# The combination of the second expert layer's rows moved unit by unit into the first steps of the last attention, with a scale of its own for four tiles

## The reference

```
    # third block, feed-forward: two experts of eight per token
    router_logits = jnp.einsum('bth,eh->bte', x, router_w)
    topk_values, topk_indices = jax.lax.top_k(router_logits, TOP_K)
    topk_weights = jax.nn.softmax(topk_values.astype(jnp.float32), axis=-1).astype(x.dtype)
    ...
    mixed_output = jnp.sum(topk_expert_outputs * topk_weights[..., None], axis=2)
    ...
    x = x + _L2_ffn_ref(_layernorm(x, axis=-1), ...)
    x = x + _L3_xattn_ref(_layernorm(x, axis=-1), ctx_1024, ...)   # 16 heads of 8, 64 tokens a sequence
    x = x + _L3_ffn_ref(_layernorm(x, axis=-1), ...)
```

## Time and profile before

| | |
|---|---|
| median of 3 runs | 1655.08 us (1648.52 to 1657.23) |
| profiled execution, its own time | 1662.0 us |
| its span in the profile | 1660.1 us |
| TensorE busy | 1342.2 us (81%) |
| VectorE busy | 1039.3 us (63%) |
| ScalarE busy | 925.4 us (56%) |
| GpSimd busy | 619.1 us (37%) |
| fetches of L1520, issue to landing | 5.7 us median, 6.8 at most |
| barrier ahead of the last attention | over at about 1270.3 us |
| first maxima of the last attention | 1282.70 us |
| last work of the last attention's steps | about 1462 us |

### The profile page before, as it was taken

One profiled execution on the slowest core, in us unless ns is written; L12 is line 12 of the kernel. 1 busy time (PEld: TensorE's weight loads), 2 busy tenths in 40 slices (PEclk: granted clock), 3 DMA queues, 4 the chain that ended last, 5 costly groups with the idle time before them and its releaser, 6 DMA issues. The chain is left out here.

```text
span 1660.1 us, 43005 instructions
## 1 busy us (share of the span) xinstructions
PE 1342.2 (81%) x16821; PEld 1121.6 (68%) x16821; DVE 1039.3 (63%) x2573; ACT 925.4 (56%) x2096; POOL 619.1 (37%) x604
## 2 busy tenths in 40 slices
PE   4799999986899997998259965777772988788994
PEld 3588877864688886787126653776661776687994
DVE  5677777764453423787879978533326788853445
ACT  3465655543345443897636634555445777634884
POOL 2233333221000000332258850677770225644662
PEclk9899999998999999898579997999995888978997
DMA  9200000009995000340000001111113001001335
GB/s 316 57 18 19 19 18 18 3 2 145 177 148 68 1 2 13 91 126 29 1 20 18 18 2 52 41 48 50 48 49 113 18 11 41 28 31 55 95 90 172
DMA packets 143528, 94.10 MB, mean 57 GB/s; under 512 B 55776, under 2 KB 130273, under 8 KB 142817
## 3 DMA queue, kind: packets, MB, share of 16 engines
q1 hardware_dynamic: 134368, 72.86, 20.3%
q0 software_dynamic: 8960, 18.50, 3.5%
HBM read 51.20 MB, written 40.12 MB: 55 GB/s over the span
## 5 line engine op out<-in xcount | busy, mean ns | idle before, releaser
L400 POOL TENSOR_TENSOR wide_probs<-wide_probs,wide_key_mask 128x512 f32<-128x512 f32 x64 | 82.7, 1315 | 187.5 <-ACT wide_probs L521 187.5
L1536 POOL DMA_INDIRECT moe_x_rows<-moe_rows,moe_source x72 | 80.5, 1118 | 74.7 <-DVE moe_source L1632 53.1
L739 POOL MEMSET attn_v_bd<- 128x576 f32 x2 | 1.2, 618 | 266.1 <-POOLq L163 266.1
L769 POOL TENSOR_TENSOR attn_col_bd<-attn_col_t,group_mask_sb 128x1024 f32<-128x1024 f32 x32 | 60.8, 1899 | 100.0 <-ACT attn_row_t L966 100.0
L2234 DVE TENSOR_TENSOR moe_hidden<-banks,moe_gate 128x256 f32<-128x256 f32 x104 | 43.6, 423 | 84.3 <-ACT moe_gate L2433 82.3
L3046 ACT ACTIVATE moe_router<-banks,moe_rb_sb 128x512 f32<-128x512 f32 x64 | 41.4, 689 | 91.7 <-PE banks L3150 67.5
L2069 POOL DMA_INDIRECT moe_results<-moe_y_rows,moe_x_rows x72 | 69.0, 958 | 51.7 <-issue 29.3
L843 DVE TENSOR_REDUCE attn_top<-banks 128x32 f32<-128x2048 f32 x32 | 73.1, 2283 | 21.0 <-PE banks L1027 21.0
L1542 POOL DMA_INDIRECT moe_results<-moe_y_rows,moe_dest x72 | 74.6, 1036 | 22.8 <-issue 20.7
L995 ACT ACTIVATE attn_probs<-attn_probs 128x1024 f32<-128x1024 f32 x64 | 66.0, 1054 | 28.3 <-DVE attn_probs L872 26.7
L2656 PE MATMUL banks<-moe_xb_t,moe_staged 128*128 128x128 f32 x576 | 76.1, 275 | 0.0
(11 more groups left out here) (434 smaller groups left out, 4362.6 us busy)
## 6 DMA issues: line engine op xcount, KB each, us to landing
moe_rows<-route_empty_sb SPq DMA_DIRECT2D x8, 2624.0 KB, 23.0
attn_ctx<-in_ctx_t SPq DMA_DIRECT2D x48, 128.0 KB, 2.1
moe_x_rows<-moe_rows SPq DMA_DIRECT2D x72, 66.0 KB, 1.9
moe_pack_sb<-in_moe_pack SPq DMA_DIRECT2D x8, 578.0 KB, 3.9
moe_w_sb<-in_moe_w SPq DMA_DIRECT2D x2, 2048.0 KB, 10.6
moe_hot<-moe_results SPq DMA_DIRECT2D x16, 256.0 KB, 5.7
moe_until_back<-moe_results SPq DMA_DIRECT2D x16, 256.0 KB, 5.9
moe_pack_sb<-in_moe_pack SPq DMA_DIRECT2D x9, 384.0 KB, 4.3
```

Of the source, the lines that this page charges most:

```text
L400: nc.gpsimd.tensor_tensor(probs[b.parity][:, :, h2], probs[b.parity][:, :, h2], keys, ALU.mult).then_inc(masked, 1)
L769: nc.gpsimd.tensor_tensor(col_bd[:], col_t[u.parity][:].unsqueeze(1).to_broadcast(shape), w["group_mask"][:].unsqueeze(2).to_broadcast(sha ...
L1536: nc.gpsimd.indirect_dma_start(x_rows[s % GATHERS][:], None, rows, bass.IndirectOffsetOnAxis(ap=source[:, s:s + 1], axis=0)).then_inc(gath ...
```

## The change

The eight units of the combination are no longer worked off by the second expert layer. SP still fetches them there, ahead of the barrier. The buffer they land in and the weights move to `core.carried`, which lives until the end; the last attention, which follows, uses the same space later for its expert blocks (`staged`, `x_rows`). Scaling, adds and bn_stats are now written into the last attention: unit 0 ahead of everything, with a norm of its own for tiles 0 to 3; units 1 to 3 behind the constant, with a norm for tiles 4 to 15; units 4 to 7 at the end of VectorE's steps 2 to 5, and behind the last a norm for tiles 16 to 31. There are three norms where there were two. ScalarE's `xhat` waits for the first, the second (from step 2) or the third (from step 8).

```
-                dve.wait_ge(y_taken, len(order))
-                dve.wait_ge(weighted, 1)
-                for u in range(UNITS):
...
+                def combine(u):
+                    part = slice(u * UNIT, (u + 1) * UNIT)
+                    dve.wait_ge(late_scaled, u + 1)
+                    nc.vector.tensor_tensor(core.x[:, part], core.x[:, part], core.late_in[:, 0, part], ALU.add).then_inc(late_half, 1)
+                    dve.wait_ge(late_half, u + 1)
+                    nc.vector.tensor_tensor(core.x[:, part], core.x[:, part], core.late_in[:, 1, part], ALU.add).then_inc(late_added, 1)
+                    dve.wait_ge(late_added, u + 1)
+                    for t in range(UNIT):
+                        ins = nc.vector.bn_stats(core.stats[:, u * UNIT + t], core.x[:, u * UNIT + t])
+                    ins.then_inc(late_stats, 1)
+
+                def first_scale(first_unit, units):
+                    tiles = slice(first_unit * UNIT, (first_unit + units) * UNIT)
+                    dve.wait_ge(late_stats, first_unit + units)
+                    norm_scale(core, dve, tiles)
+                    shifts(tiles)
...
-                shifts(FIRST_HALF)
+                combine(0)
+                first_scale(0, 1)
                 arrived(core, dve, "const", name, "moe3", "route", "dispatch")
                 dve.wait_ge(const_made, 1)
                 nc.vector.tensor_tensor(constant[:], y_of(0), w["attn3_bo"][:], ALU.add).then_inc(const_ready, 1)
-                norm_scale(core, dve, SECOND_HALF)
-                shifts(SECOND_HALF)
                 nc.vector.memset(d.seen[0][:], 0.0).then_inc(seen_made, 1)
+                for u in range(1, 4):
+                    combine(u)
+                first_scale(1, 3)
...
+                    if 4 <= s + 2 < UNITS:
+                        combine(s + 2)
+                        if s + 3 == UNITS:
+                            first_scale(4, 4)
...
+                def scale_late(u):
+                    act.wait_ge(core.late_landed[u], 2 * DMA_INC)
+                    for k in range(2):
+                        for t in range(UNIT):
+                            at = u * UNIT + t
+                            ins = nc.scalar.activation(core.late_in[:, k, at], core.late_in[:, k, at], ACT.Copy,
+                                                       scale=core.late_weight[:, k, at:at + 1])
+                    ins.then_inc(late_scaled, 1)
+
+                scale_late(0)
...
+                    if s == 1:
+                        scale_late(2)
...
                     if inside(s):
+                        act.wait_ge(norm_ready, 1 if s < 2 else 2 if s < 8 else 3)
...
+                    if s == 0:
+                        scale_late(1)
+                    elif s == 1:
+                        scale_late(3)
+                        scale_late(4)
...
+                    if 5 <= s + 3 < UNITS:
+                        scale_late(s + 3)
...
                     if inside(c):
+                        pool.wait_ge(late_added, c // 2 + 1)
```

More of the change, by code:

```diff
@@ L1484, in sparse_experts @@
         y_made, y_taken = sem("y_made"), sem("y_taken")
[L1485 to L1486 removed]
+        y_landed = core.late_landed
         rank_bank, table_bank = core.bank[7], core.bank[6]
@@ L1748, in _ @@
                         ins.then_inc(hid_ready, 1)
-                act.wait_ge(weighted, 1)
-                for u in range(UNITS):
-                    act.wait_ge(y_landed[u], 2 * DMA_INC)
-                    for k in range(1 if gated else 0, 2):
-                        for t in range(UNIT):
-                            at = u * UNIT + t
-                            ins = nc.scalar.activation(y_in[:, k, at], y_in[:, k, at], ACT.Copy, scale=weight[:, k, at:at + 1])
-                    ins.then_inc(scaled, 1)
             @block.tensor
```

57 lines of the change are left out of this document (16 added, 41 removed).

## The result

Twenty executions of each kernel on one chip: before 1655.15 us median (1647.01 to 1663.46), after 1660.73 us (1653.95 to 1668.22). The ratio is **1.0037, 95% interval [1.0022, 1.0053]**: 5.6 us slower. The likeliest case was the right one in its mechanism and too large in size: the forecast had put 0.49 on slower by more than 0.5% and 0.43 on less than that, and the measured 0.37% lies in the second.

What follows compares the result with a forecast made beforehand. VectorE was taken as the engine to count, waiting only 12.7 of 65.2 us. +8.0 at the third reciprocal, less 0.92, gave +7.1; with 1.9 for TensorE's clock +9.0, so 1664.1 us, range 1654 to 1672.

Steps and rivals of the forecast that it cites:

- The likeliest case: The forecast's own account for the whole kernel: +9.0 us, 1664.1 us, slower by 0.54%; chance 0.50.
- Start, +5.75: First add of the combination: the barrier waits for SP's 16 issues, then unit 0's scaling, so it stands 5.75 us later.
- Waits of units 1 to 3, 3.0 + 0.35 + 1.7: VectorE waits for ScalarE's scaling of units 1, 2 and 3: 3.0, 0.35 and 1.7 us.
- Holds by GpSimd, 1.9 and 1.65: GpSimd's spreads hold VectorE: the second norm for 1.9 us, unit 5's first add for 1.65 us.
- the rival in which the spreads fall between the adds: Same within 0.5%: no holds, TensorE stays at 2.4 GHz; +3.6, 1658.7 us; chance 0.26 together with the faster rival's floor.
- Third norm, +3.73: Norm behind unit 7, ahead of the third reciprocal: adds 3.73 us on VectorE.
- x waits, 1.95 and 1.25: Steps 4 and 5: x waits for ScalarE's scaling ahead of the copy of the heads; 1.95 and 1.25 us.
- Sum at the third reciprocal, +8.0: Start, third norm, new waits and holds, less the waits and hold that go: third reciprocal 8.0 us later.
- What should come back in step 6, 0.92: Step after the third reciprocal: 0.92 us returns, as old VectorE waited there for scores now ready; leaves +7.1.
- TensorE's clock, +1.9: Steps 4 and 5: pauses may drop TensorE to its lower clock; 0 to +3 us, taken as 1.9.
- Handed on: After step 6 every step hands its lateness on, through scores, subtractions, x and reciprocal: +7.1 us stays.
- lateness that shrinks over steps 7 to 19: Sign that the forecast is wrong: lateness shrinking over these later steps would mean slack it didn't see.

Runs made afterwards that it cites:

- e1: Changed kernel with only unit 0 fetched ahead of the barrier, SP issuing units 1 to 7 behind it between the first context loads: 1713.71 us, ratio to before 1.0004.
- e10: Kernel before with only a late start: VectorE fills eight dead buffers between first scaling and first add; 1659.76 us, ratio to before 1.0023.
- e4: Separate kernel computing nothing of the reference: six VectorE instructions, each alone, beside a GpSimd product and beside a GpSimd fill; no ratio to before.
- first group: The runs e0 to e3, on one chip, sharing their runs of the kernel before: median 1714.66 us (33 runs).
- e3: Changed kernel without the third norm, so tiles 16 to 31 use old mean and rstd; ratio to before 1.0043.
- e0: Changed kernel run again with no edit: 1723.27 us, ratio to before 1.0057.
- e2: Changed kernel with only one of the eight pieces of each of units 5 to 7 scaled; ratio to before 1.0047.
- e8: Kernel before run again, unchanged, against itself: 1657.77 us, ratio 1.0000.
- e9: The kernel e1 run again, in the third group of runs; ratio to before 1.0021.
- e6: The kernel e1 with the third norm's links set one by one behind the maxima and subtractions of steps 6 and 7; ratio to before 1.0024.

## Why the prediction was right, and where its size was off

*Start, +5.75.* Right: 5.59 in the trace after. The reason, SP's issues ahead of its barrier, is shown by e1 and the trace after together: with 14 of the 16 taken away the first add returns to 6.0, and in after the barrier opened 1.2 behind the last issue with transfers under way. e10 shows that such a start is handed on.

*Waits of units 1 to 3, 3.0 + 0.35 + 1.7.* 2.85, 0.28 and 1.50. In the mechanism right, 0.4 too large.

*Holds by GpSimd, 1.9 and 1.65.* 1.7 and 2.0. e4 shows the hold by itself, and the four traces of the changed order in the first group that the norm is held each time (first link to shift 5.23 or 5.24), while unit 5 is held at its first add, at its second, or not at all in e3. There, as in e0, the slow TensorE made the spread late; it began 0.09 behind the second add and took 2.36 in place of 1.89, so GpSimd was held. So one half of the rival in which the spreads fall between the adds does happen, and then TensorE's wait takes its place.

*Third norm, +3.73.* 3.66 from its start to the reciprocal; 3.5 less when e3 leaves it out.

*x waits, 1.95 and 1.25.* 1.73 and 1.44. e2 shows that the scaling ahead of the heads' copy makes the one of step 4. That of step 5 was not removed by it; there TensorE was slow.

*Sum at the third reciprocal, +8.0.* +6.9. Of the 1.1 missing, 1.0 is there already at the first max, forecast 36.2 from the fetch and measured 35.2: start 0.16, waits 0.42 and hold of the norm 0.24, the rest small. Each had been put a little high. What should come back in step 6, 0.92, measured 0.4 against the first trace of before, +6.4 at the fourth reciprocal where +7.1 was forecast. Against e8, whose step 6 is 1.2 shorter, nothing comes back: 6.6 becomes 7.4. The forecast took the old step 6 for a fixed length, and it wasn't; the new one runs its first 5 us at 1.2 GHz (granted 0.50) and has an x wait of 1.77, against 1.02 in e8.

*TensorE's clock, +1.9.* **The term that was mis-sized.** I gave a middle value to something that is there in whole or not at all, and looked for it in two steps only. In steps 4 and 5 of the trace after it is 0, in e0 it is 2.0, in e9 it adds some 1.6 to e1's 0, which makes about 0.9 as the mean of four traces, an estimate; in e3 it shows ahead of the first reciprocal (1.8), a step that the forecast gave no clock term at all. And in step 8, where the forecast expected nothing, it has the other sign: 8.05 at a granted 1.00 in after, e0, e1 and e9 against 9.4 to 9.65 in all three traces of the order before, so some 1.5 comes back. The Trainium skill, "TensorE: Matmul & The Clock Gate", section "Part 1: The HAM clock gate (the "warmup" mystery)", has the array slow when idle and fast when busy. That steps 4 and 5 would both be slow by it was the forecast's own inference, and it held in neither trace: none of the two was slow in after (granted 1.00 in both), the fifth alone in e0 (0.62). No run here shows what decides between the two.

*Handed on.* Right but for step 8. The fourteenth reciprocal in after and in e8, VectorE's timelines (first fetches at 1246.46 and 1248.61):

```profile
1447.19 0.35 DVE L2251 RECIPROCAL attn_inverse<-banks 128x32 f32<-128x32 f32 x1
```

```profile
1443.38 0.35 DVE L2271 RECIPROCAL attn_inverse<-banks 128x32 f32<-128x32 f32 x1
```

Against e8 the lateness is 7.4 at the fourth and 7.5 at the fifth reciprocal, 6.05 at the sixth, and then 5.96 to 6.04 up to the fourteenth (200.73 and 194.77 from the fetches). The forecast had named lateness that shrinks over steps 7 to 19 as a sign against it: it shrinks once, in step 8, where TensorE at its higher clock no longer lets VectorE wait. Against the first trace of before, which scatters against e8 by up to 1.7 over these steps, it is 6.4 at the fourth, 4.8 at the seventh and 4.3 to 6.3 up to the fourteenth.

*The 3.4 us that the forecast was too slow.* Against e8 the account ends at 6.0 where +9.0 was forecast. From the forecast's terms: 1.4 less at the third reciprocal, 1.9 less for a clock that stayed high in steps 4 and 5, 1.5 less in step 8, and 1.7 more in step 6. So that the point came this near owes something to luck: two misses by the clock cancel in part. The 5.6 us by medians (3.6 to 8.8 by the interval) fit the 6.0, and can't check its parts.

## What to carry to other kernels

Whoever moves work behind a barrier has to look at the queue that stays ahead of it: sixteen issues on SP cost 8.3 us, and they cost nothing only as long as other work of the stage ran beside them. Filling waits of 12.7 us didn't pay here, because the work that fills them waits for other engines itself; it brought waits for ScalarE (4.6), holds by GpSimd (3.7), a norm (3.7) and x waits (3.2), 15.2 in all. A term that is there or not, like a clock that falls, should be given as two cases with chances, not as their middle. And two traces should be compared only after a look at the clock of each: e6 looks like a loss beside e1 and like a gain beside e9, which is the same kernel as e1.

## What the runs showed of the hardware

- A VectorE scaling by a number, SBUF to SBUF, 0.23 us for 128x128, is held by a GpSimd product (1.62) and by a fill (0.65). A 128x512 add with two SBUF operands, 0.69 alone, and a fused multiply and add, 0.35, are held by a product (2.08 and 1.68) and not by a fill (0.69 and 0.35). bn_stats (0.29), an add from PSUM and SBUF and a maximum over PSUM (both 0.69) are held by neither (all in e4).
- The hold goes both ways: GpSimd's `attn_based` took 1.17 where unit 5's adds ran beside it and 0.73 in the two duos that follow, and its spread took 2.36 in e3 behind an add.
- An issue on SP costs 0.52 us (8.28 for 16), 0.46 in pairs between context loads in e1.
- The same matmuls behind a pause of 1.73 and 1.74 us ran at 2.4 GHz in one execution and at 1.2 in another. And behind the pause of 4.1 ahead of the first scores the clock came back 43.9, 46.4 and 52.4 us from the fetch in after, e0 and e3, with the same instructions ahead of it.
- The clock gives back as well as it takes: the same 32 score matmuls of step 8, behind a pause of 1.40 or 1.41, took 1.12 in after, e0, e1 and e9, and 2.02 in e8.
